# One-hots shared with ScalarE, tanh gates, shorter scatters and another order of the routing steps in a fused layer kernel

## The reference, cut to what matters

```python
off = (xn @ W_off + b_off).reshape(8, 1024, 8, 4, 2)
w   = softmax((xn @ W_attn + b_attn).reshape(8, 1024, 8, 4), axis=-1)
idx = off[..., 0].astype(int32); idx = where(idx < 0, idx + 128, idx); idx = clip(idx, 0, 127)
g   = take_along_axis(xn[:, 0, :], idx)            # values of the batch's first token
attn = broadcast(sum(g * w, heads and points)) @ W_out + b_out
logits = xn @ router_w.T + expert_bias             # 8 experts
rw, sel = top_k(logits, 2); rw = softmax(rw)       # two gates per token
ffn = sum of 2 shared experts + sum over the two chosen experts of rw * (silu(xn@w1.T) * (xn@w3.T)) @ w2.T
```

## Time and profile before

| | us |
|---|---|
| median of 3 runs | 404.47 |
| the profiled execution | 404.78 |
| its span in the trace | 403.0 |
| PE busy | 361.8 (90%) |
| VectorE busy | 313.6 (78%) |
| ScalarE busy | 181.0 (45%) |
| POOL busy | 233.1 (58%) |

### The profile page before, as it was taken

One profiled execution on the slowest core, in us unless ns is written; L12 is line 12 of the kernel. 1 busy time (PEld: TensorE's weight loads), 2 busy tenths in 40 slices (PEclk: granted clock), 3 DMA queues, 4 the chain that ended last, 5 costly groups with the idle time before them and its releaser, 6 DMA issues.

```text
span 403.0 us, 12432 instructions
## 1 busy us (share of the span) xinstructions
PE 361.8 (90%) x4303; PEld 311.7 (77%) x4303; DVE 313.6 (78%) x863; ACT 181.0 (45%) x420; POOL 233.1 (58%) x200
## 2 busy tenths in 40 slices
PE   0166898897999999999999999999999999999992
PEld 0065666574677777777779999999999999999992
DVE  4988889887989899999986678666666666666662
ACT  2667845677233566666667444222222222222220
POOL 1556801167777643343204999278866677666776
PEclk9999999999999999999999999999999999999997
DMA  8954630001128668787884566766664755452333
GB/s 291 294 129 105 129 84 2 0 29 56 49 65 160 147 132 166 158 163 152 161 132 79 161 190 162 136 83 63 71 59 60 64 63 63 58 60 28 30 34 32
DMA packets 99013, 41.34 MB, mean 103 GB/s; under 512 B 73744, under 2 KB 92560, under 8 KB 98960
## 3 DMA queue, kind: packets, MB, share of 16 engines
q1 hardware_dynamic: 87264, 31.82, 37.7%
q0 software_dynamic: 11264, 8.69, 16.1%
q10 hardware_dynamic: 432, 0.11, 0.2%
HBM read 10.94 MB, written 12.88 MB: 59 GB/s over the span
## 4 chain that ended last, share of the span: by engine, by line
PE 76%; DVE 9%; SPq 4%; POOL 3%; issue 3%; ACT 3%; DMA 2%; DVEq 0%; POOLq 0%; ACTq 0%
PE pY L853 18%; PE pY L686 12%; PE pAB L829 9%; PE pAB L828 9%; PE pAB L827 9%; PE pAB L674 5%; PE pAB L676 5%; PE pAB L675 5%; PE pV L698 4%; SPq L493 2%; DMA xT<-hot 2%; DVE hbuf L1259 2%; SPq L487 1%; POOL hot L1065 1%; POOL units L1073 1%
## 5 line engine op out<-in xcount | busy, mean ns | idle before, releaser
L1121 POOL DMA_INDIRECT out_dram<-xT,rows x64 | 98.9, 1545 | 47.5 <-DVE xT L1617 22.2
L1109 POOL DMA_INDIRECT sorted_rows<-rows,slot x64 | 66.9, 1046 | 58.9 <-DVE hbuf L1259 46.2
L1052 ACT ACTIVATE units<-pAB 128x512 f32<-128x512 f32 x78 | 46.4, 594 | 109.9 <-PE pAB L829 109.1
L827 PE MATMUL pAB<-rows,wsp 128*128 128x128 f16 x512 | 87.6, 219 | 0.0
L829 PE MATMUL pAB<-rows,wsp 128*128 128x128 f16 x512 | 87.6, 219 | 0.0
L828 PE MATMUL pAB<-rows,wsp 128*128 128x128 f16 x512 | 87.6, 219 | 0.0
L1555 DVE SCALAR_TENSOR_TENSOR hbuf<-pAB,units 128x512 f32<-128x512 f32 x78 | 53.5, 686 | 37.7 <-PE pAB L829 36.8
L853 PE MATMUL pY<-wsp,hbuf 128*128 (+1 forms) x620 | 78.9, 279 | 0.4 <-issue 0.4
L853 PEld LDWEIGHTS pY<-wsp,hbuf 128*128 128x128 f32 x620 | 72.7, 192 | 0.9 <-issue 0.7
L686 PE MATMUL pY<-wsp,hbuf 128*128 128x128 f32 x512 | 70.3, 280 | 0.0
L686 PEld LDWEIGHTS pY<-wsp,hbuf 128*128 128x128 f32 x512 | 64.3, 192 | 4.0
(11 more groups left out here) (165 smaller groups left out, 606.0 us busy)
## 6 DMA issues: line engine op xcount, KB each, us to landing
base<-in_x SPq DMA_DIRECT2D x8, 512.0 KB, 7.3
out_dram<-base SPq DMA_DIRECT2D x16, 256.0 KB, 2.4
wraw<-in_wall SPq DMA_DIRECT2D x10, 256.0 KB, 3.0
rows<-hot SPq DMA_DIRECT2D x8, 256.0 KB, 2.8
proj<-sorted_rows SPq DMA_DIRECT2D x27, 68.5 KB, 1.8
wsp<-in_wall SPq DMA_DIRECT2D x10, 128.0 KB, 3.5
sorted_rows<-rows,slot POOLq DMA_INDIRECT x64, 2.5
out_dram<-xT,rows POOLq DMA_INDIRECT x64, 3.3
```

Source lines behind the costliest of these rows:

```text
L827: pe.matmul(o, hi, x(0), start=True, stop=False)
L1109: pool.indirect_dma_start(sorted_rows, bass.IndirectOffsetOnAxis(ap=slot[:, t:t + 1].bitcast(U32), axis=0), rows[:, t, :], None, bounds_ch ...
L1121: pool.indirect_dma_start(out_rows, bass.IndirectOffsetOnAxis(ap=meta[:, t, DEST - CW:DEST - CW + 1].bitcast(U32), axis=0), yt[:, t], None ...
```

## The change

- The gates come from tanh: 0.5 + 0.5 tanh(gap/2) and 0.5 - 0.5 tanh(gap/2), in place of an exponential, an addition, a reciprocal and a product.
- The routing steps of VectorE are in another order: the clip of the offsets before the places, the words right behind the table of tiles without a unit between them, the table ahead of the indices. Places, segments, table and Abs move by a unit or two on TensorE and ScalarE.
- The one-hots of 0 and 15 are written by ScalarE, as relu(1 - v) and relu(v - 14); VectorE does the other 14 in portions of 5, 5, 4, 0.
- `pick(n-3)` stands ahead of `first_products(n)`; `weigh` and `sums` have one unit more of lag.
- Experts 2 to 5 are split at units 32 to 35, the other four at units 39, 47, 55 and 63; their loads use one buffer.
- A scatter has no bound check, no wait for an earlier scatter and no increment of `pool_go`.

```diff
-GAP_UNIT, COLUMN_UNIT, STEP_UNIT, PLACE_UNIT = 7, 10, 10, 11
-SEG_UNIT, TAB_UNIT, TABLE_UNIT, SIDES_UNIT = 14, 19, 22, 26
-LOGIT_UNIT, ABS_UNIT, WHOLE_UNIT, SIGN_UNIT = 16, 15, 18, 20
+GAP_UNIT, COLUMN_UNIT, STEP_UNIT, PLACE_UNIT = 7, 10, 10, 12
+SEG_UNIT, TAB_UNIT, TABLE_UNIT, SIDES_UNIT = 15, 18, 20, 26
+LOGIT_UNIT, ABS_UNIT, WHOLE_UNIT, SIGN_UNIT = 16, 14, 19, 20
+EARLY_SPLITS = 4
+HOT_OPS = [(1, 6), (6, 11), (11, 15), (15, 15)]
...
+        "edge": np.broadcast_to(np.array([1.0, 2.0 - LO16], f32)[None, :], (P, 2)),
...
-                sp.dma_start(wraw[:, e % 2, 0:W2], wall[e, :, 0:W2]).then_inc(w_in[e % 2], 16)
+                r = e % 2 if e < NSH + EARLY_SPLITS else 0
+                sp.dma_start(wraw[:, r, 0:W2], wall[e, :, 0:W2]).then_inc(w_in[r], 16)
...
+                    sp.wait_ge(hot_edges, m // 4 + 1)
...
-                if m % 4 == 3 and 2 * NSH + m // 4 < NE:
-                    e = 2 * NSH + m // 4
-                    sp.wait_ge(w_split, e - 1)
+                if m == 3:
+                    for e in range(2 * NSH, NSH + EARLY_SPLITS):
+                        sp.wait_ge(w_split, e - 1)
+                        load_first(e)
+                if m % 8 == 7 and NSH + EARLY_SPLITS + m // 8 < NE:
+                    e = NSH + EARLY_SPLITS + m // 8
+                    sp.wait_ge(w_split, e - 1 if m == 7 else e)
                     load_first(e)
...
-            both = shared[:1] + [(2, pick, ROUND * ATT, UNITS)] + shared[1:]
+            both = [(3, pick, ROUND * ATT, UNITS)] + shared
...
-                    nc.scalar.activation(rt[:, 5, :], rt[:, 4, :], ACT.Exp).then_inc(gap_exp, 1)
+                    nc.scalar.activation(rt[:, 5, :], rt[:, 4, :], ACT.Tanh, scale=0.5).then_inc(gap_tanh, 1)
...
+                if isinstance(g, int) and g == ATT and u < EARLY_SPLITS:
+                    split_high((NSH + u) // 2, u % 2)
+                if u == 7:
+                    act.wait_ge(w_in[0], 16 * g)
+                    nc.scalar.activation(whi[:, bass.ds(g + 2, 1), 0:W2].rearrange("p o c -> p (o c)"),
+                                         wraw[:, 0, 0:W2], ACT.Copy, scale=WS).then_inc(w_split_hi, 1)
+
+            def hot_edge(g, u):
+
+                batch = 2 * (g - ATT) + (u // 4 + 1)
+                if u % 4:
+                    return
+                if past(batch, 2):
+                    for r in range(TURNS):
+                        act.wait_ge(hot_turned[r], 16 * (batch - 1))
+                src = proj_i16[:, bass.ds(TPS * batch, TPS), 0:HP].rearrange("p t (g h) -> p t g h", h=GRP)
+                for n, k in enumerate((0, LO16 - 1)):
+                    a = nc.scalar.activation(hot[:, (u // 4 + 1) % 2, :, :, k, :], src, ACT.Relu,
+                                             bias=c["edge"][:, n:n + 1], scale=2.0 * n - 1.0)
+                a.then_inc(hot_edges, 1)
...
+            both = shared + [(4, sums, ROUND * ATT, UNITS), (0, hot_edge, ROUND * ATT + 4, UNITS - 4), (0, bias_rows, ROUND * ATT, UNITS),
...
-                if t >= OUT_SEMS:
-                    pool.wait_ge(d_out[t % OUT_SEMS], 16 * (t // OUT_SEMS))
-                pool.sem_inc(pool_go, 1)
                 pool.indirect_dma_start(out_rows, bass.IndirectOffsetOnAxis(ap=meta[:, t, DEST - CW:DEST - CW + 1].bitcast(U32), axis=0),
-                                        yt[:, t], None, bounds_check=TOK - 1, oob_is_err=False,
-                                        compute_op=ALU.add).then_inc(d_out[t % OUT_SEMS], 16)
+                                        yt[:, t], None, compute_op=ALU.add).then_inc(d_out[t % OUT_SEMS], 16)
...
-            then(v.tensor_scalar(rt[:, 6, :], rt[:, 5, :], 1.0, None, ALU.add))
-            then(v.reciprocal(rt[:, 8, :], rt[:, 6, :]))
-            v.tensor_tensor(rt[:, 9, :], rt[:, 8, :], rt[:, 5, :], ALU.mult).then_inc(cw_pair, 1)
+            v.tensor_scalar(rt[:, 8, :], rt[:, 5, :], -0.5, 0.5, ALU.mult, ALU.add)
+            v.tensor_scalar(rt[:, 9, :], rt[:, 5, :], 0.5, 0.5, ALU.mult, ALU.add).then_inc(cw_pair, 1)
...
+                lo, hi = HOT_OPS[u % 4]
+                for k in range(lo, hi):
                     ins = v.tensor_scalar(hot[:, (u // 4 + 1) % 2, :, :, k, :], src, float(k), None, ALU.is_equal)
...
-            both = shared_parts[:1] + [(0, one_hot, start + 4, end - 4), (2, weigh, start, end),
+            both = shared_parts[:1] + [(0, one_hot, start + 4, end - 4), (3, weigh, start, end),
```

More of the change, by code:

```diff
@@ L439, in layer_kernel @@
         hot_ready = sem("hot_ready")
+        hot_edges = sem("hot_edges")
         aw_ready = sem("aw_ready")
@@ L1015, in routed_high, with first_edges @@
             def routed_high(g, u):
-                if u % 4 == 1:
-                    split_high(g - (ATT - 1), u // 4)
+                if isinstance(g, int) and g == ATT and u < EARLY_SPLITS:
[16 more added lines that the diff above has]
+                a.then_inc(hot_edges, 1)
+            def first_edges(g, u):
+                n = ROUND * g + u
+                if n == ROUND * ATT - 8:
+                    act.wait_ge(scratch_free, 1)
+                if n >= ROUND * ATT - 8:
+                    hot_edge(g + u // 4, (u + 4) % ROUND)
             shared = [(0, silu_unit, 0, UNITS)]
-            routing = shared[:1] + [(0, exponentials, 0, UNITS)] + shared[1:]
-            both = shared + [(3, sums, ROUND * ATT, UNITS), (0, bias_rows, ROUND * ATT, UNITS),
+            routing = shared + [(0, exponentials, 0, UNITS), (0, first_edges, 0, UNITS)]
+            both = shared + [(4, sums, ROUND * ATT, UNITS), (0, hot_edge, ROUND * ATT + 4, UNITS - 4), (0, bias_rows, ROUND * ATT, UNITS),
                              (0, routed_high, ROUND * ATT, UNITS)]
@@ L1026, in _ @@
             straight(ROUND * ATT, ROUND * (ATT + 1), both)
-            rounds(act, ATT + 1, UNITS // ROUND, both)
-            straight(UNITS, UNITS + 3, both)
+            rounds(act, ATT + 1, UNITS // ROUND - 1, both)
+            straight(UNITS - ROUND, UNITS + 4, both)
             def r_xt(g, r):
@@ L1384, in _ @@
             v.tensor_copy(tab16[:], tab_f[:, 0:2]).then_inc(tab_ready, 1)
+            assert unit[0] == TAB_UNIT - 1
+            dve.wait_ge(tab_done, 1)
+            part = lambda k, h: pV[0:1, 0, (k + 2) * P + h * WORDS:(k + 2) * P + (h + 1) * WORDS]
+            for h in range(2):
+                v.tensor_scalar(words[:, h, :], part(1, h), float(2 ** FIELD), None, ALU.mult)
+                then(v.tensor_copy(words[:, 2 + h, :], part(0, h)))
+            for h in range(2):
+                then(v.tensor_tensor(words[:, h, :], words[:, h, :], words[:, 2 + h, :], ALU.bitwise_or))
+            then(v.tensor_scalar(words[:, 1, :], words[:, 1, :], 2 * HALF * FIELD, None, ALU.logical_shift_left))
+            then(v.tensor_tensor(words[:, 0, :], words[:, 0, :], words[:, 1, :], ALU.bitwise_or))
+            v.memset(seg[:, 2, 1:2], 0.0).then_inc(tsel_ready, 1)
             shared_unit()
@@ L1404, in _ @@
             shared_unit()
[L1406 to L1416, removed]
+            assert unit[0] > TABLE_UNIT
+            dve.wait_ge(table_done, 1)
+            same = c["same_gather"][:].unsqueeze(1).broadcast_to([P, 8, HI16 * GRP])
+            for k in range(2):
+                ins = v.tensor_tensor(table[:, 4 * k:4 * k + 4].rearrange("p b s c -> p (b s) c"),
+                                      pV[:, k, :].rearrange("p (g c) -> p g c", g=8), same, ALU.mult)
+            ins.then_inc(table_ready, 1)
             shared_unit()
@@ L1431, in _ @@
             shared_unit()
[L1433 to L1440, removed]
             def one_hot(g, u):
@@ L1449, in one_hot @@
                 src = proj_i16[:, bass.ds(TPS * batch, TPS), 0:HP].rearrange("p t (g h) -> p t g h", h=GRP)
-                for k in range(LO16 // 4 * (u % 4), LO16 // 4 * (u % 4 + 1)):
+                lo, hi = HOT_OPS[u % 4]
+                for k in range(lo, hi):
                     ins = v.tensor_scalar(hot[:, (u // 4 + 1) % 2, :, :, k, :], src, float(k), None, ALU.is_equal)
-                if u % 4 == 3:
+                if lo < hi == LO16 - 1:
                     ins.then_inc(hot_ready, 1)
@@ L1485, in routed_low @@
             def routed_low(g, u):
-                if u % 4 == 2:
-                    split_low(g - (ATT - 1), u // 4)
+                if isinstance(g, int) and g == ATT and u < EARLY_SPLITS:
+                    split_low((NSH + u) // 2, u % 2)
+                if u == 7:
+                    dve.wait_ge(w_split_hi, g + 3)
+                    row = lambda a: a[:, bass.ds(g + 2, 1), 0:W2].rearrange("p o c -> p (o c)")
+                    v.scalar_tensor_tensor(row(wlo), wraw[:, 0, 0:W2], WS, row(whi), ALU.mult, ALU.subtract).then_inc(w_split, 1)
             def extra_table():
```

11 lines of the change are left out of this document (6 added, 5 removed).

## The result

The changed kernel takes 399.43 us (median of 4 runs, 399.26 to 399.89), and beside it the kernel before took 404.7 us: a ratio of 0.987 with an interval of 0.985 to 0.989. The forecast was 399.8. The profiled execution took 399.35 us with a span of 397.5, against 404.78 and 403.0.

A forecast was written before the change was run, and what follows sets the result against it. PE was taken to bind attention with VectorE 1% behind, with holes in routing and a queue of scatters at the end. Terms -2.6 - 2.5 + 0.3 + 0.8 - 0.7 = -4.7 us gave 399.8 us, range 397.6 to 402.9.

The forecast's parts named there:

- Gates: Routing: tanh in place of the exponential gates costed at nothing; at most 0.7 us gain if not covered.
- The cover named: Routing: VectorE's step after the gates waits for TensorE's column sums anyway, 0.35 us idle, so shorter gates gain nothing.
- Order of routing: Routing, units 11 to 24: reordered VectorE steps start unit 24 at 105.3 instead of 107.84 us, -2.6 us.
- the walk: Step-by-step estimate of routing units 11 to 24, using delays from the earlier profile, behind the -2.6 us.
- The first rival, holes that only move: Routing: each wait removed returns at the next hf unit, giving 402.4 us; chance 0.12.
- Pick ahead: Attention: second products return to 0.89 us, a unit falls from 2.74 to 2.66 us, 29 times, -2.5 us.
- +0.3 for weigh: Attention: room before a pick needs weigh shrinks to 0.8 us; allowance for places where it doesn't fit, 0 to +2.
- The rival of the weight load: Attention: the weight load behind picks still shows, giving 402.3 us; chance 0.08.
- End of attention: Unit 63: split and add_shared delay weigh 29, so pick 31 waits; +0.8 us, 0 to +2.
- Scatters: Tail: 0.1 us off each scatter, plus 0.1 to 0.2 for the wait and increment, -0.7 us (0 to -1.9).
- The cheap-scatter rival: Tail: the bound check is most of a scatter's cost, giving 398.6 us; chance 0.12.
- Slower rival: Attention: pick ahead makes PE wait for weigh in each unit, +5.6 us, giving 405.4 us; chance 0.06.

The follow-up runs named there:

- pool_late: Changed kernel with the old exponential gates, and POOL's combine-weight products held back until VectorE has read the first half of the places: 399.3 us.
- gates_exp: Changed kernel with only the gates put back to exponential, addition, reciprocal and product: 400.28 us.
- pick_only: Kernel before with only picks moved ahead of first products, weigh and sums one unit later: 404.85 us, ratio 1.0003.
- pick_old: Changed kernel with picks back between first and second products, weigh and sums at their old lags: 400.71 us.
- splits_old: Changed kernel with expert loads and splits as before, one split in four units and none at units 32 to 35: 399.24 us.
- split_six: Changed kernel with the last four splits one unit earlier (38, 46, 54, 62) and their loads two picks earlier: 399.36 us.
- hot_vector: Changed kernel with all 16 comparisons on VectorE, four a unit, and none on ScalarE: 401.7 us.
- scatter_waits: Changed kernel with the scatters' wait for an earlier scatter and the increment put back, without the bound check: 400.6 us.
- gates_table: Changed kernel with only ScalarE's tanh turned back to the exponential, VectorE's two short steps kept: 399.2 us.

## Why the prediction was right, step by step

The two profiled executions are 5.44 us apart against 4.7 forecast, and the medians taken side by side 5.27. That 399.43 comes within 0.4 of 399.8 is helped a little by where the forecast set out: 404.47, where the median beside the result is 404.7.

- **Gates: 0 forecast, -0.73 to -0.84 measured. This is the term that was mis-sized.** The cover named, the wait for the column sums, was there. The row beside it was read past: the earlier trace rows show the copy at 69.42, and the step behind it took 1.06 us for 28 elements, which by its size is far too long. It was POOL's work that made it so, and the gates release POOL. The forecast's bound "at most 0.7" comes near the measured number, but by luck: it was the gates' own length, and pool_late keeps that length and loses nothing.
- **Order of routing: -2.6 forecast, -2.3 to -2.4 measured.** First products of unit 24 start at 104.42 against 105.3 forecast: the gates and the head's 0.28 make it 1.0 earlier, and the order itself gives 0.2 less than forecast. In gates_exp, with the old gates as in the walk, they start at 105.10. The new wait at L624's second half, forecast at 1.0, is 0.8 in gates_exp, and the gates take it away in the kernel after. The walk took all of the 1.74 us before L624 for the order's; 0.7 of it was the gates'. The first rival, holes that only move, is out.
- **Pick ahead: 2.74 to 2.66 forecast, 2.65 measured**; -2.5 for it and +0.3 for weigh stand against -2.10 in 35-63 and 0.09 more from unit 34 to 35. Of the late weighs little shows: the steps at units 41 and 42 are 2.68 and 2.81, all others 2.65 to 2.67. ScalarE's two new activations take 0.50 us each, within the bounds of 0.2 to 0.6. The rival of the weight load is out, by 0.89 in place of 0.97. pick_only shows what the forecast only said in passing: the term needs two edits at once. The pick alone gains nothing, and the relief alone nothing either (35-63 is 76.58 in pick_old as before).
- **End of attention: +0.8 forecast, 0.77 of wait and +0.93 over all.** The mechanism was that named: without the late split (splits_old, split_six) all of the 0.93 is gone.
- **Scatters: -0.7 forecast, -0.79 measured, and the reason was wrong, so that the number fits is luck.** The forecast took 0.1 off each scatter's duration and expected them 1.7 us apart; they are 1.85 apart as before. The other half, tile 60's lateness, is what went, and more of it, since each scatter that finds POOL idle starts 0.6 us sooner. The cheap-scatter rival is out. The rule of the Trainium skill that the prediction sets against this term (DMA: Bandwidth & Descriptors, section "Anatomy of one DMA — SWDGE (gpsimd) path") would have had no gain. The tail gained, but not in the 1.54 us that POOL is busy, which no edit moved, so the rule is neither borne out nor refuted.
- **Slower rival:** out for the full change. hot_vector shows that it comes, in the units behind a split, when VectorE keeps its comparisons. (Its sum in the prediction, 29 x (2.85 - 2.66), is 5.5 and not 5.6.)

## What to carry to other kernels

Where two engines are within 1% of each other, as here, an edit that shortens one may be worth nothing until the other is lightened too; price them as one term and test each alone. Look in a timeline for an instruction that is long for its size, before costing what stands beside it as covered: its length may be set by another engine's work. Ahead of a DMA that waits for a result, look for further instructions on that queue: here one of 29 ns counted, and a second beside it added hardly anything. And look at the granted clock of every trace before comparing its stretches.

## What had not been expected of the hardware

- POOL's products of 128x512 made VectorE's step of 28 elements take 1.06 us in place of 0.19, and the maxima 1.78 in place of 1.22.
- A MOVE of 29 ns, or a wait and an increment of a semaphore, ahead of an indirect DMA puts its start 0.51 or 0.55 us later where POOL had been idle (1.13 and 1.17 in place of 0.62 us), and nothing in a queue of scatters (0.30 us between two in all four traces).
- TensorE's granted clock fell to 0.5 for 3.4 us of routing in one of the 14 traces (scatter_waits, 93.36 to 96.78 us) and cost 1.3 us.
- Tanh beside silu needs no table load. From unit 4 on, ScalarE loads tables in the kernel after only around the softmax's exponential (1.28 us at 86.10 and at 89.32); gates_table has two at the gates as well, and its time is the same.
